# Feed-forward stage with routed experts: the order planner's batch price, the spacing instruction on GpSimd and the place of the second layer's shared and gate items

## What is computed

```python
x = x + attn_a(layernorm(x), ...)          # 16 heads, (q k)^4, causal
x = x + ffn(layernorm(x), gate_w, w1, w2, shared_w1, shared_w2)
x = x + attn_b(layernorm(x), ...)          # silu of a convolution along the batch axis, per feature
x = x + ffn(layernorm(x), ...)             # the same weights

def ffn(x):                                # T tokens, 16 experts, 6 of them per token
    shared_out = silu_and_mul(x @ shared_w1.T) @ shared_w2.T      # inner width 352
    probs = softmax(x @ gate_w.T)
    weights, selected = top_k(probs, 6)
    moe = sum over the 6: weight * (silu_and_mul(x @ w1[e].T) @ w2[e].T)   # inner width 176
    return moe + shared_out
```

## Time and profile before

| | |
|---|---|
| median of 3 runs | 2266.47 us (2265.01 to 2270.17) |
| the profiled execution | 2266.18 us, of which 2264.4 us from the first to the last instruction |
| PE | 1991.5 us busy, 88% |
| POOL | 1453.3 us busy, 64% |
| DVE | 1420.7 us busy, 63% |
| ACT | 1221.7 us busy, 54% |
| TensorE's granted clock | 0.93 of full speed on the mean |

### The profile page before, as it was taken

The page is one execution under the profiler, slowest core; times in us unless marked ns, Lnnn a source line. Parts: engine busy times, 40 slices in busy tenths (PEclk is TensorE's granted clock), DMA queues, the critical chain, the costliest instruction groups (busy, mean ns, idle before and its releaser), DMA issues.

```text
span 2264.4 us, 43979 instructions
## 1 busy us (share of the span) xinstructions
PE 1991.5 (88%) x11798; PEld 1393.7 (62%) x11798; DVE 1420.7 (63%) x3810; ACT 1221.7 (54%) x3024; POOL 1453.3 (64%) x2052
## 2 busy tenths in 40 slices
PE   5878999999768999999999997899994597899896
PEld 4434544444336777777777776676773476676674
DVE  3758787777866874444787442687762263647656
ACT  2565666575746555555556554455652354454452
POOL 1435545354853888885870188898468588828647
PEclk8798989798977999999999999899997799899998
DMA  4296779644425546665654365566642465656533
GB/s 115 44 230 135 193 201 227 143 104 83 85 83 162 171 145 212 203 203 166 184 179 143 97 201 180 166 195 194 191 151 111 151 213 179 201 163 206 178 96 100
DMA packets 262467, 361.45 MB, mean 160 GB/s; under 512 B 51553, under 2 KB 226977, under 8 KB 261537
## 3 DMA queue, kind: packets, MB, share of 16 engines
q1 hardware_dynamic: 224608, 256.35, 40.6%
q0 software_dynamic: 36864, 100.71, 13.7%
q10 hardware_dynamic: 768, 1.57, 0.5%
HBM read 209.34 MB, written 180.22 MB: 172 GB/s over the span
## 4 chain that ended last, share of the span: by engine, by line
POOL 33%; PE 26%; issue 5%; DVE 3%; DMA 2%; ACT 1%; SPq 0%; POOLq 0%; ACTq 0%; DVEq 0%
POOL rows L1329 14%; PE ffn_psum L1751 14%; POOL spaced L1304 10%; POOL xs L1314 8%; PE ffn_psum L1780 7%; PE ffn_psum L1760 2%; PE ffn_psum L1719 2%; DMA xin<-xs 1%; DMA rows<-ys,idx 0%; POOL f_rstd L1292 0%; DMA ys<-yo 0%; PE ffn_psum L1732 0%; PE ffn_psum L1796 0%; PE ffn_psum L1794 0%; DVE al L1524 0%
## 5 line engine op out<-in xcount | busy, mean ns | idle before, releaser
L1751 PE MATMUL ffn_psum<-w,xt 128*128 (+1 forms) x2152 | 742.0, 468 | 10.9 <-issue 10.4
L1780 PE MATMUL ffn_psum<-wd,ah 128*128 (+1 forms) x1806 | 452.2, 319 | 64.0 <-DVE al L1524 63.4
L1329 POOL DMA_INDIRECT rows<-ys,idx x384 | 378.8, 986 | 168.8 <-DMA ys<-yo 108.6
L1751 PEld LDWEIGHTS ffn_psum<-w,xt 128*128 128x128 f32 x2152 | 371.0, 192 | 140.3 <-issue 28.0
L1355 ACT ACTIVATE sg<-ffn_psum 128x176 f32<-128x176 f32 x602 | 190.8, 317 | 463.8 <-PE ffn_psum L1751 462.9
L1524 DVE TENSOR_TENSOR al<-ffn_psum,ah 128x256 fp32r<-128x256 f32 x602 | 254.3, 422 | 238.5 <-ACT ah L1362 229.8
L470 DVE TENSOR_TENSOR a<-a 128x1024 f32<-128x1024 f32 (+2 forms) x304 | 329.7, 1110 | 91.2 <-ACT a L366 90.6
L1314 POOL DMA_INDIRECT xs<-xn,idx x288 | 288.2, 1001 | 128.2 <-DVE idx L1572 81.1
L1780 PEld LDWEIGHTS ffn_psum<-wd,ah 128*128 128x128 f32 x1806 | 305.4, 193 | 89.4 <-issue 57.2
L366 ACT ACTIVATE a<-attn_psum 128x1024 f32<-128x1024 f32 (+1 forms) x320 | 290.3, 942 | 123.3 <-PE attn_psum L690 122.5
L1304 POOL TENSOR_TENSOR spaced<-f_ident 128x128 f32<-128x128 f32 x768 | 333.8, 435 | 18.2
(11 more groups left out here) (193 smaller groups left out, 2652.0 us busy)
## 6 DMA issues: line engine op xcount, KB each, us to landing
xin<-xs SPq DMA_DIRECT2D x474, 128.0 KB
ys<-yo SPq DMA_DIRECT2D x474, 128.0 KB
acc<-x SPq DMA_DIRECT2D x24, 512.0 KB, 4.4
qt<-by_head SPq DMA_DIRECT2D x42, 256.0 KB, 8.9
kt<-by_head SPq DMA_DIRECT2D x42, 256.0 KB, 8.2
xs<-x SPq DMA_DIRECT2D x3, 2944.0 KB, 20.3
by_head<-sq SPq DMA_DIRECT2D x14, 512.0 KB, 6.1
by_head<-cs SPq DMA_DIRECT2D x14, 512.0 KB, 7.9
```

The costliest lines, as they stand in the source:

```text
L1329: pool.indirect_dma_start(rowset(q, b)[:, k, :], None, ys[g % 3][0:NBK[g] * P, :], bass.IndirectOffsetOnAxis(at, 0)).then_inc(s_rows[j % 4 ...
L1751: last = pe.matmul(GU(n)[:, 0:wide], x[:, k * P:(k + 1) * P], of(k), start=k == 0, stop=k == KE - 1)
L1780: last = pe.matmul(Y(m), a[:, part * P:part * P + P], of(i), start=opens and j == 0, stop=closes(n) and j == len(terms) - 1, skip_group_ch ...
```

## The change

The planner charges a batch with 4.05 units in place of 3.5. The spacing instruction is a memset of 128x256 elements, no longer a tensor_tensor over 128x128. All second-layer tiles are now in `GATE_FIRST`: their logits come from short items as soon as the tile is normalized, and their S items wait in `soon`. Those of tiles 8 to 11 are taken when no R item is ready, or when a first-layer tile's statistics are held up by them (`hindered`). The buffer of a normalized tile may only be overwritten when its S items have been planned too, and ACT waits for the transposes of the last of them. The groups stay as they were. POOL's wait for the identity's load is gone, since the memset doesn't read it.

```diff
@@ -790,6 +790,8 @@
     def allowed(job):
         kind = job[0]
         if kind == "stat":
+            if job[1] == 1 and not all(p in shared_at and landed.get(group[p], 1e9) <= t for p in holder(job[2])):
+                return False
             return sum(k[0] == "norm" and pos[k] < n for k in pos) > len(order) - 4
@@ -797,8 +799,15 @@
     def free(q):
 
-        held = [p for p in (*range(4), *range(NT, q + NT)) if p % 5 == (q + NT) % 5][-1:]
-        return all(landed.get(group[p], 1e9) <= t for p in held)
+        return all(landed.get(group[p], 1e9) <= t and shared_at.get(p, 1e9) < n - 1 for p in holder(q))
+
+    def holder(q):
+
+        return [p for p in (*range(4), *range(NT, q + NT)) if p % 5 == (q + NT) % 5][-1:]
+
+    def hindered():
+
+        return any(j[3][:2] == ("stat", 1) and j[0] <= t + 2 and any(p not in shared_at for p in holder(j[3][2])) for j in jobs)
@@ -875,7 +884,7 @@
-            elif soon:
+            elif soon and (q <= NT or not (left and landed.get(left[0][1], 1e9) + 3 <= t) or hindered()):
                 item = soon.pop(0)
@@ -960,7 +969,7 @@
                 pool.append((what, q, b))
-                pool_t += 3.5
+                pool_t += 4.05
@@ -1002,7 +1011,7 @@
         PUT_OFF = range(TT - 4, TT)
-        GATE_FIRST = (*GROUPS[0], *PUT_OFF)
+        GATE_FIRST = (*GROUPS[0], *range(NT, TT))
@@ -1050,7 +1059,7 @@
-        spaced = sb("spaced", [P, P])
+        spaced = sb("spaced", [P, 2 * P])
@@ -1280,7 +1289,6 @@
-            pool.wait_ge(s["const"], 16)
@@ -1301,7 +1309,7 @@
-                pool.tensor_tensor(spaced[:], ident[:], ident[:], ALU.add).then_inc(s["space"], 1)
+                pool.memset(spaced[:], 0.0).then_inc(s["space"], 1)
@@ -1397,6 +1405,7 @@
                         for p in [p for p in (*range(4), *range(NT, q + NT)) if p % 5 == (q + NT) % 5][-1:]:
                             act.wait_ge(s_sc[GROUP[p]], SCATTERED[GROUP[p]])
+                            act.wait_ge(s["t"], XIX(S_LAST[p]) + 1)
```

## The result

The changed kernel took 2619.7 us (median of 4 runs, 2602.32 to 2625.39) beside 2268.3 us of the kernel before (2265.01 to 2271.76): a ratio of 1.154, 95% interval 1.148 to 1.159. It is 351 us slower, where 2198 was forecast. Run again unaltered, the same program took 2192.5 us, then 2194.2, and then 2632.5. The first two of these lie within 6 us of the forecast, the last is this result once more. The document is about that split.

The account below looks back on a forecast made before the run. The prediction had PE bound most stages, slowed by DVE's too-early adds, and POOL bound group 4's scatters and the last gathers. Stage savings of 68.2 us took the 2264.4 us span to 2196.2, so 2198 us; range 2170 to 2240.

Parts of the forecast that it names:

- POOL's other 648 spacing instructions: Spacing outside the two POOL-bound stages: shortening it changes no time, as it lies beside PE-bound work.
- Rival 3: Adds on DVE: its own work, not late rows, is the stall, so 2272 us, slower than before; chance 0.06.
- Start to group 4's scatters: First 953.8 us of items: 15.5 us more short-item work against 33 us of stalls saved, net -17.6 us.
- Group 4's scatters: POOL-bound stage of 122.3 us: 72 spacing instructions, each 0.13 us shorter, -9.4 us.
- Group 4's R items: PE-bound stage of 246.9 us: 32.6 us of stalls cut to 9, -23.6 us.
- Group 5's R items: PE-bound stage of 154.5 us: 15.4 us of stalls cut to 4, -11.4 us.
- Last gathers: POOL-bound end of 84.9 us: 48 shorter spacing instructions, -6.2 us.
- Spacing instruction: POOL's spacing between indirect DMAs: 0.305 us as a memset, from 0.435, saving 0.8 us a batch.
- DVE's waits for rows: DVE's waits for gathered rows, 14.04 us at tile 9: under 3 us each in the PE-bound stages.
- Rival 1: DVE's multiply-add bursts stay long, 22 us more, 2220 us; chance 0.20 together with the rival on new holds.
- Rival 2: The memset still takes 0.435 us and the bursts stay long: 2252 us; chance 0.08.
- Rival 4: New holds in the order lose half of the first stage's 33 us: 2215 us; 0.20 with the long-bursts rival.

Follow-up runs that it names:

- e5: The changed kernel, unaltered, run again on chip 14: 2192.5 us, ratio 0.968.
- e11: The kernel before with only the planner's price of a batch raised from 3.5 to 4.05 items: 2218.5 us, ratio 0.976.
- e12: The kernel before with price 4.05 and the memset on 256 columns, without the new order's rules: 2191.3 us, ratio 0.964.
- e1: The changed kernel with the old spacing instruction (tensor_tensor over 128x128) and POOL's wait for the identity: 2231.6 us, ratio 0.982.
- e2: The kernel before with the memset of 128x256 as spacing instruction, its only change: 2207.2 us, ratio 0.972.
- e8: The kernel before with the memset of 256 columns and without the wait for the identity's load: 2200.0 us, ratio 0.971.
- round 4: Chip 2: changed kernel unaltered 2632.5 us, without spacing instruction 2895.2; kernel before with 128-column memset at price 4.05 2814.4, at 3.7 2807.2.
- stepped run: Two runs: kernel before, price 4.05, memset width stepped down to 256 columns within group 0's scatters; 336 columns elsewhere 2188.1 us, 400 elsewhere 2206.5.
- e10: The changed kernel with the memset on 128 columns in place of 256, on chip 1: 2180.6 us, ratio 0.962.

## Why the prediction was wrong, and where it was right

**The step that failed** is the one that cost the closer indirect DMAs at nothing: "POOL's other 648 spacing instructions lie beside PE-bound work." As a sum of durations that is so, and on chips 4, 14 and 1 it held. In the result the stretch up to group 4's scatters, which was to become 17.6 us shorter, became 267 longer. On chip 2, and on the occasion of the result, which had the same time and the same marks in its trace, PE's signals come microseconds late (2.0 us in the median, 5.11 at the item above) while POOL issues indirect DMAs 1.46 us apart or closer. An item passes from PE to ACT's sg and DVE's ac, back to PE, then to ACT's ah and DVE's al and back again. Its second product stands behind two of PE's signals, and PE's next items behind that. The rows of before could not show it: they hold the old distance only, 1.59 us for scatters and 1.55 for gathers, at which no such thing occurs. The forecast had the spacing instruction as a thing that only costs time.

**Rival 3**, the one that ended slower, had DVE's adds as the stall. That was not it: PE is slow from 790 us on, and the first add of a gathered row starts at 1219.5 us in that execution.

**Where chips are undisturbed, the steps can be held against e5** (span 2190.2 us, forecast 2196.2). The instructions that ended the long waits there:

```profile
1631.21 1.07 POOL L1322 DMA_INDIRECT xs<-xn,idx  x1 [12.79 <-DVE idx L1581]
...
1741.70 0.66 PE L1728 MATMUL ffn_psum<-f_ident,xin 128*128 128x128 f32 x2 [45.44 <-DMA xin<-xs]
...
1968.07 0.95 POOL L1337 DMA_INDIRECT rows<-ys,idx  x1 [46.59 <-DMA ys<-yo]
...
2109.49 0.95 POOL L1337 DMA_INDIRECT rows<-ys,idx  x1 [36.09 <-DMA ys<-yo]
```

- Start to group 4's scatters: 1631.2 us, forecast 1638; -24.6 against -17.6. The kept stalls or the short items were put too high; which isn't split.
- Group 4's scatters: 110.5 us to PE's return, against 122.3: -11.8, forecast -9.4.
- Group 4's R items: 226.4 against 246.8 us: -20.4, forecast -23.6.
- Group 5's R items: 141.4 against 154.6 us: -13.2, forecast -11.4.
- Last gathers: 80.7 against 84.9 us: -4.2, forecast -6.2.
- Sum -74.2, forecast -68.2.
- Spacing instruction 0.329 us, forecast 0.305. An indirect DMA is 1.46 us behind the one before (scatter) or 1.44 (gather), so a batch is 8.7 to 8.8 us, where 8.7 to 9.0 was forecast. Its own terms (9.3 and 9.5 less 0.8) give 8.5 and 8.7, so the reading was a little high, and the longer memset made up for it.
- DVE's waits for rows: 9.0 us in all, of which 8.8 lie in the last gathers, which POOL bounds; in the other stages they come to 0.2 us, where under 3 us each was forecast.

**Rival 1, that the bursts stay long**, fell. With the old instruction the median of a large group of adds is 619 ns even at the new price (e11), with the memset it is 479 (e12), beside indirect DMAs all the same. The adds' mean over all 368 is 544 ns with the tensor_tensor and 480 with the memset. The Trainium skill, SBUF — State Buffer, section Who interferes with whom, has a VectorE instruction with two SBUF inputs contend with a GpSimd instruction that reads SBUF, not with one that only writes. These traces agree. **Rival 2, spacing not shorter**, fell with 0.329 us. **Rival 4, the new holds**, has no cost beside the memset and perhaps 13 us with the old instruction (e1 against e11).

**The weight of the parts was not as argued, and the 2198 is in part luck.** Of its 68 us the sum gave 38 to the memset (15.6 to the shorter spacing, 22 to the shorter adds). Rival 2, which is price and order with the old spacing, stood at 2252 us, 14 under the kernel before. That program was run as e1: 2231.6, 41 under. The step from there to the changed kernel was put at 54 us and came to about 32 to 39 (by the ratios and by the times, on two chips). So the plan was valued too low and the memset on top of it too high, and the two errors nearly cancel. Alone, the price gives 53 us and the memset 66 (e2 and e8), together 80 and not 119. In part both remove the same waits of DVE for rows: 64.2 us before, 13.8 with the price, 41.7 with the memset, 6.9 with both. That overlap is 16 of the 39 us; the rest wasn't traced. The order's rules give nothing.

## What stays open

Why PE's signals come late on one chip is not shown. Something that takes up updates at a limited rate, and falls behind when the indirect DMAs add theirs too fast, would do it, and the slow onset fits that; so would anything else of that chip that POOL's indirect DMAs load more there. One rival was not tested at all: every execution on record, timed ones included, carries a recorded span and clock, so no time without the profiler's recording stands beside these. Whether the recording has a part in it can't be told; a third and more of its update records are missing in the long traces, most of them of DMAs (15 of the 17 thousand that the result's trace lacks). Nor is it shown that distance acts alone (round 4), nor is the edge known, nor how many chips have it (one of the six occasions here had it, and the result's own did too). Whether a memset at 1.58 us is safe on chip 2 was not tried there, since neither stepped run came to it; that the kernel before is safe at 1.59 is measured in every round. No version is known to beat both kernels on all chips. On the undisturbed ones e10 is the fastest at 2180.6 us, and e12 reaches the changed kernel's time with four edited lines. The candidate to try first on chip 2 is the price alone (e11, 0.976): it leaves POOL's distance as it was.

## What to carry to other kernels

A planner's price that agrees with the measured duration of a batch was worth more here than rules around it: one number, 3.5 to 4.05, gave 53 us, and 80 with a spacing instruction that doesn't read SBUF. An instruction that is there to space others is a limit set by hand, and shortening it is a change of its own with a risk of its own: test it on several chips, and keep the plan's part apart from it. When a time is far from a sum of durations that the trace confirms one by one, run the unaltered program again elsewhere before explaining it.

## What the hardware showed unexpectedly

On one chip (and on the occasion of the result) the time of every kernel run went with the distance between POOL's indirect DMAs: 2268 us at 1.59, 2632 at 1.46, about 2810 at 1.35, 2895 at 1.26. On the others nothing of the kind was seen at 1.46, and on the one of them where 1.35 was run (chip 1) it was faster still. In the result's trace POOL's and DVE's instructions and the DMA packets keep their durations, and DVE's al, which waits for ACT, starts at most 0.10 us behind it. Late is what waits for PE (ACT's sg 5.13 us behind the end of its product, in place of 0.03). About 28 to 30 thousand of 44.8 thousand semaphore updates are in the long traces. TensorE's granted clock falls in those stretches, behind its own idle time (0.77, 0.75, 0.59 and 0.52 in the four long traces shown, from 860 to 930 us).
